# New places for the side stages among 32 scan units, and a last stage that sums four parts behind, in SBUF

## The chip, the cores and the metric

The kernel runs on one core of one Trainium2 chip. The metric is the device time of one execution in microseconds. Its engines are TensorE (PE in the rows; PEld is its weight load), VectorE (DVE), ScalarE (ACT), GpSimd (POOL) and SyncE (SP), which only issues transfers here.

## The reference, cut to what matters

For 32 sequences of 512 tokens with 256 features, in float32:

```
x = x + layernorm(A(layernorm(x)))        # A: a state space block and an attention-like block
x = x + layernorm(F(layernorm(x)))        # F: 8 experts, top 2, capacity 2048 per expert

A:  u, res = split(x @ in_w);  u = silu(conv4(u));  dt, B, C = split(u @ xp_w)
    delta = softplus(dt @ dt_w + dt_b);  dA[t,d,n] = exp(delta * -exp(A_log))
    h[t] = dA[t] * h[t-1] + delta[t] * u[t] * B[t]          # 512 channels x 16 states
    y = sum_n(h * C) + u * D;  m = (y * silu(res)) @ out_w
    h = ln(m + x); q, k; G = sum over tokens of (weights * q); hs = ((G * k) @ proj * ln(h)) @ fl
    h2 = ln(hs + h);  out = ln(gelu(h2 @ d1) @ d2 + h2)
F:  router softmax of the top 2, the first 2048 tokens of each expert kept, relu(x @ w1) @ w2,
    times the router's weight, added back at the token's row
```

The last stage computes `out = x1 + layernorm(F's rows)` for each token, `x1` being the result of the first line.

## The kernel before, in words

It has three phases, one behind the other.

**The attention phase** takes one sequence at a time through a scan. The 512 channels are four chunks of 128 partitions, and the 16 states go in pairs, so a sequence has 4 x 8 = 32 units. In unit k VectorE runs one `tensor_tensor_scan` over two states of 512 steps (L1111) and makes the next unit's input with one multiply, `drive` (L1084; at a chunk's start also `du`, L1079). ScalarE makes the decays of unit k+1 with two exponentials (L745), GpSimd multiplies unit k-1 with C (L529, `times_c`), and TensorE adds unit k-2 into the PSUM tile `y` (L920, preceded at a chunk's start by the skip term, L917). At the end of a chunk VectorE's `gate` (L1090) takes `y` times the gate into `u`. `st` has four buffers, so scan k waits for TensorE's sum of unit k-4; `dA` has two, so the decays of unit k+1 wait for scan k-1. SyncE loads the rows of B and C of unit k+2 (L369), with two buffers for B and four for C.

Beside the scan of sequence b run the side stages of three others: `late` of b-2, `post` of b-1 and `pre` of b+1. `pre` normalises, projects, convolves and makes delta. `post` does all from the output projection to the first half of the feed-forward (d1 and gelu). `late` does its second half (d2), the last normalisations, the first residual, the router, and scatters the tokens to the experts' rows by indirect transfers from GpSimd.

The order on each engine is written out by hand. A sequence has 96 slots, three for a unit. In every slot an engine first does its own piece of the scan and then what the stages have for this slot. VectorE has nothing in slot 3k, scan k in slot 3k+1, `drive` of unit k+1 in slot 3k+2. ScalarE has one decay of unit k+1 in 3k and one in 3k+1, GpSimd `times_c` of unit k-1 in 3k+1, TensorE the sum of unit k-2 in 3k+2, SyncE the row loads of unit k+2 in 3k. What is left of the scan (TensorE's sums 30 and 31, GpSimd's product 31) comes behind slot 95. Each stage is a generator that yields the slot of its next piece from a list `at`:

```python
def run_to(self, slot):
    while self.slot is not None and self.slot <= slot:
        self.slot = next(self.instructions, None)
...
            for slot in range(SLOTS * NU):
                if parts is not None:
                    parts[slot % SLOTS](slot // SLOTS)
                for stage in stages:
                    stage.run_to(slot)
```

The stages of one slot come in the order gates, late, post, pre. Between engines there are only semaphores. Nothing plans these places at build time: the lists `at` are all there is. Two sequences form one turn of a hardware loop (14 turns for sequences 2 to 29), the others stand before and behind it.

Names that the text uses: on VectorE `f_sum0`, `f_sum1` (L1186), `f_g` (L1194, which reads the power `r_late` of GpSimd, L473), the second statistics, `dots` (L1208); "t" (L1165, which reads TensorE's projection `hs` and SyncE's receipt L434); `delta0`, `delta2` (L1066); conv (L1061). On TensorE `m0`, `m1` (output projection), `d2_0` to `d2_3` (all L866), `d1` in four pairs (L992), the turns (L858). On GpSimd `s_g`, `s_b` and the small instructions of a layernorm: a negated mean, variance plus epsilon, a power of -1/2 on 128x4 (L473, L497), a product.

**The expert phase** runs four turns of two experts. It isn't touched.

**The last stage** (`combine_phase`) takes 32 parts of 512 tokens. A part is loaded by SyncE into one of eight tiles `rows` (128x1024), VectorE takes its statistics (L1555, L1560), GpSimd makes scale and shift (L1587 to L1592), ScalarE normalises in four instructions (L1616), the sum with `x1_all`, which lies in SBUF, goes to VectorE for even parts (L1568) and to GpSimd for odd ones (L1601), and ScalarE issues the store (L1623). Even parts are normalised into four PSUM tiles `normed`, odd ones in place. The sum of part n-2 stands ahead of the statistics of part n on VectorE, and ahead of scale and shift of part n on GpSimd; the store of part n-2 behind the normalisation of part n.

Of the kernel before, what the change touches and what calls it, by code (L numbers as in the profile page):

```python
# [12 lines left out]
P = 128  # L13
# [97 lines left out]
def attention_phase(nc, t, env, sem):  # L111
# [14 lines left out]
    with ExitStack() as ctx:  # L126
# [225 lines left out]
        def _(sp):  # L352
# [19 lines left out]
            def pre(b, par):  # L372
                at = iter((2, 16, 52, 64, 95))
# [37 lines left out]
            def post(b, par, more):  # L411
                at = iter((4, 52))
# [13 lines left out]
            def late(b):  # L426
                at = iter((38, 58))
# [13 lines left out]
        def _(pool):  # L441
# [61 lines left out]
            def pre(b, par):  # L503
                at = iter((11, 16, 67, 69, 70, 73))
# [45 lines left out]
            def post(b, par, more):  # L550
                at = iter((13, 19, 22, 34, 37, 41, 53, 53, 61, 70))
# [34 lines left out]
            def late(b):  # L586
                at = iter((0, 1, 18, 20, 22, 27, 29, 43, 43, 45, 45, 45, 45, 48, 51))
# [37 lines left out]
        def _(act):  # L625
# [37 lines left out]
            def pre(b, par):  # L663
                at = iter((10, 14, 17, 17, 19, 19, 25, 36, 43, 43, 48, 55, 59, 59, 59, 60, 61, 62, 65, 66, 69, 92))
# [97 lines left out]
            def post(b, par, more):  # L762
                at = iter((12, 20, 35, 35, 35, 35, 37, 53, 64, 73, 76, 86, 95))
# [57 lines left out]
            def late(b):  # L821
                at = iter((22, 25, 25, 30, 36, 42))
# [26 lines left out]
        def _(pe):  # L849
# [20 lines left out]
            def pre(b, par):  # L870
                at = iter((20, 25, 25, 25, 36, 38, 46, 46, 47, 49, 52, 52, 55, 55))
# [58 lines left out]
            def post(b, par, more):  # L930
                at = iter((1, 2, 24, 26, 26, 44, 48, 54, 61, 67, 76, 78, 83, 84, 88))
# [64 lines left out]
            def late(b):  # L996
                at = iter((0, 10, 10, 13, 38, 38, 45))
# [32 lines left out]
        def _(dve):  # L1030
# [20 lines left out]
            def pre(b, par):  # L1051
                at = iter((20, 28, 33, 39, 82, 88, 95))
# [40 lines left out]
            def gates(b, par):  # L1093
                at = iter((30, 56, 77))
# [28 lines left out]
            def post(b, par, more):  # L1123
                at = iter((2, 11, 11, 27, 31, 44, 49, 58, 68))
# [53 lines left out]
            def late(b):  # L1178
                at = iter((13, 18, 18, 18, 40, 40, 42))
# [300 lines left out]
def combine_phase(nc, t, env, sem):  # L1480
# [3 lines left out]
    with ExitStack() as ctx:  # L1484
# [4 lines left out]
        H = 4  # L1489
# [6 lines left out]
        normed = [ctx.enter_context(nc.psum_tensor(f"normed{i}", [P, TT, D], F32)) for i in range(H)]  # L1496
# [11 lines left out]
        c_out_dve = Steps(sem("c_out_dve"), range(0, G, 2))  # L1508
        c_out_pool = Steps(sem("c_out_pool"), range(1, G, 2))
        c_out = [c_out_dve, c_out_pool]  # L1510
# [35 lines left out]
        def _(dve):  # L1546
# [16 lines left out]
            def add(n, i):  # L1563

                if n % 2:
                    return
                dve.wait_ge(*c_normed.at(n, i))
                dve.tensor_tensor(x1_of(n, i), normed[n // 2 % H][:, :, :].rearrange("p t d -> p (t d)"), x1_of(n, i), ALU.add)\  # L1568
                    .then_inc(c_out_dve.did(n), 1)

            turns(dve, ((2, add), (0, stats)))

        @block.gpsimd
        def _(pool):
# [20 lines left out]
            def add(n, i):  # L1595

                if n % 2 == 0:
                    return
# [5 lines left out]
            turns(pool, ((2, add), (0, scale_and_shift)))  # L1604

        @block.scalar
        def _(act):
            c_normed.credit(act)

            def normalise(n, i):  # L1610
                act.wait_ge(*c_shift.at(f"shift{n}", i))
                if n % 2 == 0:
                    act.wait_ge(*(c_out_dve.at(n - 2 * H, i) if n >= 2 * H else c_out_dve.at((n - 2 * H) % G, i - 1)))
                for tile in range(TT):
                    src = rows[n][:, tile, :]
                    last = act.activation(src if n % 2 else normed[n // 2 % H][:, tile, :], src, ACT.Identity,  # L1616
                                          bias=shift[n][:, tile:tile + 1], scale=r[n][:, tile:tile + 1])
                last.then_inc(c_normed.did(n), 1)

            def store(n, i):  # L1620
                act.wait_ge(*c_out[n % 2].at(n, i))
# [4 lines left out]
            turns(act, ((0, normalise), (2, store)))  # L1626
# [35 lines left out]
```

## Time and profile before

| | us |
|---|---|
| three timed runs | 6304.99, 6323.98, 6331.19 |
| median | 6323.98 |
| the profiled execution, its own time | 6312.81 |
| its span in the trace | 6311.1 |
| VectorE busy, whole span | 5058.4 (80%) |
| TensorE busy | 5337.9 (85%) |
| GpSimd busy | 4465.4 (71%) |
| ScalarE busy | 3688.4 (58%) |
| first and last start of a scan (L1111) | 69.1 and 5468.6 |
| first statistics of the last stage | 6180.3 |

The attention phase is the stretch of the scans and some 100 us behind them. A wait in the rows is the idle time of an engine just before an instruction, with what ended it; "issue" is a wait for nothing that the profile shows, as at the jump of a loop.

### The profile page before, as it was taken

What the parts mean: (1) busy time and instruction counts of PE and PEld (TensorE: products, weight loads), DVE (VectorE), ACT (ScalarE), POOL (GpSimd) and SP (SyncE); (2) the same over time, 40 slices, a digit from 0 to 9 for tenths busy, and PEclk for the clock granted to TensorE, in tenths of its full rate; (3) what the DMA queues carried; (4) which work ended last, traced back from release to release, by engine and by line L of the source; (5) the groups of instructions that cost most, each with busy time, mean ns of one, the idle gap of its engine ahead of it and who ended that gap; (6) DMA issues with size and microseconds to landing.
All of it is one profiled execution on the core that took longest, in us unless ns stands there. A gap on an engine that the chain in (4) does not pass through costs nothing. (4 is left out here: it accounts for less than half of the span.)

```text
span 6311.1 us, 71449 instructions
## 1 busy us (share of the span) xinstructions
PE 5337.9 (85%) x16896; PEld 2976.5 (47%) x16896; DVE 5058.4 (80%) x6651; ACT 3688.4 (58%) x6370; POOL 4465.4 (71%) x3013
## 2 busy tenths in 40 slices
PE   5788888888888888988888888888898888749990
PEld 2344444444444444444444444444444444436660
DVE  5888989998889899898888999988898898612224
ACT  5566666666666666666666666666666665321114
POOL 3677777777777777777777777777777777523446
PEclk8899999999999999999999999999999999869995
DMA  7876666666666666666666666666665666405556
GB/s 223 277 244 228 227 229 228 235 226 219 223 220 226 222 222 223 220 226 222 224 217 227 218 218 216 220 212 218 218 219 201 222 220 213 145 27 119 122 109 220
DMA packets 486058, 1316.23 MB, mean 209 GB/s; under 512 B 54687, under 2 KB 194976, under 8 KB 485552
## 3 DMA queue, kind: packets, MB, share of 16 engines
q1 hardware_dynamic: 441424, 1242.65, 58.4%
q0 software_dynamic: 30720, 34.17, 3.0%
q10 hardware_dynamic: 13408, 34.08, 1.4%
q14 instruction: 361, 2.96, 0.2%
q8 instruction: 145, 2.38, 0.2%
HBM read 1189.94 MB, written 138.02 MB: 210 GB/s over the span
## 5 line engine op out<-in xcount | busy, mean ns | idle before, releaser
L529 POOL TENSOR_TENSOR st<-st,C_rows 128x1024 f32<-128x1024 f32 x1024 | 2478.7, 2427 | 520.1 <-DVE st L1111 509.9
L1111 DVE TENSOR_TENSOR_SCAN st<-dA,drive 128x1024 f32<-128x1024 f32 x1024 | 2338.9, 2284 | 242.4 <-PE y L920 117.1
L920 PE MATMUL y<-st,ident 128*128 128x512 f32 x4096 | 1974.4, 620 | 171.6 <-POOL st L529 168.4
L745 ACT ACTIVATE dA<-delta,a_neg 128x511 f32<-128x511 f32 x2048 | 1367.8, 712 | 706.8 <-DVE st L1111 698.1
L920 PEld LDWEIGHTS y<-st,ident 128*128 128x128 f32 x4096 | 793.3, 199 | 1193.7 <-issue 865.4
L1084 DVE TENSOR_TENSOR drive<-du,B_rows 128x1024 f32<-128x1024 f32 x1024 | 1260.2, 1231 | 107.5 <-DVE du L1079 20.7
L889 PE MATMUL pre_bank<-e_abs,in_w 128*128 128x512 f32 x1024 | 587.9, 715 | 86.2 <-DVE u L1061 78.1
L866 PE MATMUL post_bank<-d_w,gT 128*128 128x256 f32 x2048 | 464.2, 383 | 30.3 <-issue 29.6
L617 POOL DMA_INDIRECT expert_in<-tb,idx x256 | 271.8, 1062 | 264.0 <-DVE idx L1266 190.7
L866 PEld LDWEIGHTS post_bank<-d_w,gT 128*128 128x128 f32 x2048 | 391.9, 192 | 129.0 <-issue 77.1
L1427 POOL DMA_INDIRECT token_rows<-O,dest_i x128 | 198.1, 1547 | 307.2 <-DVE O L1474 219.9
L889 PEld LDWEIGHTS pre_bank<-e_abs,in_w 128*128 128x128 f32 x1024 | 214.5, 223 | 351.2 <-issue 206.3
L1061 DVE SCALAR_TENSOR_TENSOR u<-pre_bank,conv_w,u 128x511 f32<-128x511 f32 (+2 forms) x384 | 285.8, 744 | 23.7 <-ACT u L690 14.7
L992 PE MATMUL post_bank<-F,d_w 128*128 128x512 f32 x512 | 245.9, 625 | 2.5 <-ACT F L811 1.5
L858 PE MATMUL post_bank<-ident,tb 128*128 128x128 f32 x768 | 116.7, 301 | 142.3 <-ACT tb L646 109.0
L866 PE MATMUL post_bank<-F,gT 128*128 128x256 f32 x512 | 153.1, 466 | 98.2 <-ACT F L799 98.2
L1377 PE MATMUL bank<-XT,w 128*128 128x512 f32 x512 | 227.8, 598 | 5.3 <-ACT XT L1402 5.3
L1387 PE MATMUL bank<-w,I 128*128 128x256 f32 x1024 | 228.6, 381 | 3.3 <-issue 3.3
L992 PE MATMUL pre_bank<-F,d_w 128*128 128x512 f32 x512 | 230.2, 592 | 0.0
L866 PE MATMUL pre_bank<-out_w,u 128*128 128x256 f32 x1024 | 226.4, 379 | 2.5 <-issue 2.5
L1474 DVE TENSOR_SCALAR O<-bank,w_slot 128x256 f32<-128x256 f32 x128 | 53.1, 477 | 213.9 <-PE bank L1387 213.9
L1410 ACT ACTIVATE I<-bank 128x512 f32<-128x512 f32 x64 | 38.2, 597 | 316.6 <-PE bank L1377 316.6
(210 smaller groups left out, 8048.9 us busy)
## 6 DMA issues: line engine op xcount, KB each, us to landing
B_rows<-bc_rows SPq DMA_DIRECT2D x1024, 512.0 KB
C_rows<-bc_rows SPq DMA_DIRECT2D x1024, 512.0 KB, 5.1
expert_in<-zeros ACTq DMA_DIRECT2D x22, 768.0 KB, 5.5
X<-expert_in SPq DMA_DIRECT2D x32, 528.0 KB, 4.8
xin<-in_x SPq DMA_DIRECT2D x32, 512.0 KB, 6.9
xn_rows<-xin SPq DMA_DIRECT2D x32, 512.0 KB, 3.3
token_rows<-zeros SPq DMA_DIRECT2D x32, 512.0 KB, 7.4
h<-xn_rows SPq DMA_DIRECT2D x32, 512.0 KB, 7.8
```

The lines of the kernel that those rows point to most:

```text
L529: pool.tensor_tensor(tile[:, :, :], tile[:, :, :], bc[1][k % ROWS[1]][:, :, :], ALU.mult)\
L617: pool.indirect_dma_start(out=xe_dram, out_offset=bass.IndirectOffsetOnAxis(ap=idx[:, tile, choice:choice + 1], axis=0), in_=tb_wide[:, ti ...
L745: return act.activation(dA[k % 2][:, j, 1:L], delta[par][:, c, 1:L], ACT.Exp, scale=a_neg[:, c, n:n + 1])
L866: last = pe.matmul(banks[tile // 2][:, (tile % 2) * D:(tile % 2 + 1) * D], srcT[:, c, tile * P:(tile + 1) * P], w[:, c, :], start=c == 0, ...
L889: last = pe.matmul(RB[m % 2][:, :], in_w[:, c, m * P:(m + 1) * P], xT[:, c, :], start=c == 0, stop=c == KD - 1)
L920: last = pe.matmul(Y[:, :], ident[:, :], st[k % RING][:, j, :], start=False, stop=pair == CU - 1 and j == 1)
L992: last = pe.matmul(FB[j % 4][:, :], d1_w[:, c, j * P:(j + 1) * P], F[:, c, :], start=c == 0, stop=c == KD - 1)
L1061: dve.scalar_tensor_tensor(late, RB[c % 2][:, 0:L - 1 - j], conv_w[:, c, 2 - j:3 - j], late, ALU.mult, ALU.add).then_inc(pre_dve.did(f"con ...
L1084: dve.tensor_tensor(DR[:, :, :], DU[:, :].unsqueeze(1).to_broadcast([P, 2, L]), bc[0][k % ROWS[0]][:, :, :], ALU.mult).then_inc(scan_in.di ...
L1111: dve.tensor_tensor_scan(st[k % RING][:, :, :].rearrange("p a l -> p (a l)"), dA[k % 2][:, :, :].rearrange("p a l -> p (a l)"), DR[:, :, : ...
L1377: last = pe.matmul(MB[m][:, 0:BLK], w1[e][:, c, m * P:(m + 1) * P], XT[n % 2][:, c, :], start=c == 0, stop=c == KD - 1)
L1387: last = pe.matmul(OB[tile // 2][:, (tile % 2) * D:(tile % 2 + 1) * D], I[n % 2][:, c, tile * P:(tile + 1) * P], w2[e][:, c, :], start=c = ...
```

## The change

Every list `at` of the attention phase gets other numbers; the pieces and their order within a stage stay. In the last stage `normed` goes, ScalarE normalises every part in place, the sum follows four parts behind, and GpSimd has one sum of four, VectorE three.

```diff
 sync     pre   (2, 16, 52, 64, 95)                     -> (4, 39, 86, 95, 95)
          post  (4, 52)                                 -> (1, 35)
          late  (38, 58)                                -> (25, 51)
 gpsimd   pre   (11, 16, 67, 69, 70, 73)                -> (12, 14, 78, 80, 86, 88)
          post  (13, 19, 22, 34, 37, 41, 53, 53, 61, 70)
             -> (18, 27, 32, 36, 47, 48, 50, 65, 67, 78)
          late  (0, 1, 18, 20, 22, 27, 29, 43, 43, 45, 45, 45, 45, 48, 51)
             -> (10, 11, 21, 24, 27, 28, 32, 41, 41, 41, 45, 45, 45, 47, 48)
 scalar   pre   (10, 14, 17, 17, 19, 19, 25, 36, 43, 43, 48, 55, 59, 59, 59, 60, 61, 62, 65, 66, 69, 92)
             -> (9, 11, 14, 14, 18, 31, 32, 47, 50, 53, 60, 65, 65, 65, 66, 66, 71, 73, 74, 74, 83, 95)
          post  (12, 20, 35, 35, 35, 35, 37, 53, 64, 73, 76, 86, 95)
             -> (16, 22, 28, 32, 38, 40, 40, 56, 69, 76, 78, 88, 94)
          late  (22, 25, 25, 30, 36, 42)                -> (26, 28, 29, 34, 34, 40)
 tensor   pre   (20, 25, 25, 25, 36, 38, 46, 46, 47, 49, 52, 52, 55, 55)
             -> (11, 17, 29, 31, 39, 44, 47, 51, 52, 55, 61, 61, 61, 63)
          post  (1, 2, 24, 26, 26, 44, 48, 54, 61, 67, 76, 78, 83, 84, 88)
             -> (5, 5, 20, 25, 29, 36, 50, 59, 65, 68, 80, 83, 86, 89, 95)
          late  (0, 10, 10, 13, 38, 38, 45)             -> (0, 11, 11, 11, 36, 36, 39)
 vector   pre   (20, 28, 33, 39, 82, 88, 95)            -> (31, 37, 43, 44, 95, 95, 95)
          gates (30, 56, 77)                            -> (32, 55, 75)
          post  (2, 11, 11, 27, 31, 44, 49, 58, 68)     -> (0, 9, 10, 26, 34, 48, 49, 65, 73)
          late  (13, 18, 18, 18, 40, 40, 42)            -> (12, 18, 19, 20, 38, 39, 40)
```

```diff
-        H = 4
+        LAG = 4
-        normed = [ctx.enter_context(nc.psum_tensor(f"normed{i}", [P, TT, D], F32)) for i in range(H)]
+        c_out_dve = Steps(sem("c_out_dve"), [n for n in range(G) if n % 4 != 1])
+        c_out_pool = Steps(sem("c_out_pool"), [n for n in range(G) if n % 4 == 1])
             def load(n, i):
-                if n % 2:
-                    sp.wait_ge(*c_out_pool.at(n, i - 1))
-                else:
-                    sp.wait_ge(*c_normed.at(n, i - 1))
+                sp.wait_ge(*c_out(n).at(n, i - 1))
             def add(n, i):                                  # VectorE
-                if n % 2:
+                if n % 4 == 1:
                     return
-                dve.tensor_tensor(x1_of(n, i), normed[n // 2 % H]..., x1_of(n, i), ALU.add)
+                dve.tensor_tensor(x1_of(n, i), rows[n]..., x1_of(n, i), ALU.add)
-            turns(dve, ((2, add), (0, stats)))
+            turns(dve, ((LAG, add), (0, stats)))
             def add(n, i):                                  # GpSimd
-                if n % 2 == 0:
+                if n % 4 != 1:
                     return
-            turns(pool, ((2, add), (0, scale_and_shift)))
+            turns(pool, ((LAG, add), (0, scale_and_shift)))
             def normalise(n, i):
-                if n % 2 == 0:
-                    act.wait_ge(*(c_out_dve.at(n - 2 * H, i) if ... else ...))
-                    last = act.activation(src if n % 2 else normed[n // 2 % H][:, tile, :], src, ...)
+                    last = act.activation(src, src, ...)
-            turns(act, ((0, normalise), (2, store)))
+            turns(act, ((0, normalise), (LAG, store)))
```

## Rows read from the trace of the kernel before

**Rows 1.** Windows: us, then busy us (x instructions) per engine, PEclk, DMA share, GB/s

```profile
2000.00:3000.00 1000.00, 881.87 (x2760) 481.38 (x2759) 894.78 (x1087) 654.58 (x1133) 772.52 (x504) 0.95 0.66 224
```

**Rows 2.** Groups by line, 1000 to 3000 us: busy us, mean ns, idle before

```profile
L1111 DVE TENSOR_TENSOR_SCAN st<-dA,drive 128x1024 f32<-128x1024 f32 x379 | 865.8, 2284 | 87.9 <-PE y L920 45.8 <-issue 13.3 <-ACT dA L745 13.0
...
L694 ACT ACT_TABLE_LOAD x11 | 14.1, 1283 | 0.2
```

**Rows 3.** Timeline of VectorE, one unit with nothing beside it: start, us, what

```profile
3060.30 1.23 DVE L1084 TENSOR_TENSOR drive<-du,B_rows 128x1024 f32<-128x1024 f32 x1
...
3064.02 1.23 DVE L1084 TENSOR_TENSOR drive<-du,B_rows 128x1024 f32<-128x1024 f32 x1
```

**Rows 4.** Waits of VectorE, 1000 to 5000 us: total us, times, longest

```profile
DVE st L1111 <- PE y L920: 86.2, 64, 2.9
DVE post_bank L1194 <- POOL r_late L473: 38.0, 24, 1.6
DVE st L1111 <- ACT dA L745: 33.5, 50, 3.3
DVE tb L1165 <- PE post_bank L866: 32.9, 15, 3.3
DVE st L1111 <- issue: 27.7, 11, 3.9
...
DVE tb L1165 <- SPq L434: 17.0, 9, 2.0
...
DVE drive L1084 <- issue: 1.0, 5, 0.2
```

**Rows 5.** Timeline of VectorE around the late stage

```profile
3118.01 2.29 DVE L1111 TENSOR_TENSOR_SCAN st<-dA,drive 128x1024 f32<-128x1024 f32 x1 [0.84 <-ACT dA L745]
...
3125.81 1.67 DVE L1194 SCALAR_TENSOR_TENSOR post_bank<-post_bank,mv_late,row_ln_g 128x256 f32<-128x256 f32 x4 [1.58 <-POOL r_late L473]
```

**Rows 6.** Timeline of VectorE around "t"

```profile
3034.78 1.66 DVE L1165 SCALAR_TENSOR_TENSOR tb<-post_bank,rk,row_pr_b 128x256 f32<-128x256 f32 x4 [2.12 <-PE post_bank L866]
...
3039.39 2.29 DVE L1111 TENSOR_TENSOR_SCAN st<-dA,drive 128x1024 f32<-128x1024 f32 x1 [1.82 <-PE y L920]
```

**Rows 7.** Timeline of the last stage: GpSimd at its start, VectorE's sums later

```profile
6182.65 0.25 POOL L1587 TENSOR_SCALAR c_shift<-c_mv 128x4 f32<-128x4 f32 x1 [6.08 <-DVE c_mv L1560]
...
6184.70 0.23 POOL L1587 TENSOR_SCALAR c_shift<-c_mv 128x4 f32<-128x4 f32 x1
...
6270.42 1.23 DVE L1568 TENSOR_TENSOR x_all<-normed,x_all 128x1024 f32 x1 [2.73 <-ACT normed L1616]
...
6278.14 1.22 DVE L1568 TENSOR_TENSOR x_all<-normed,x_all 128x1024 f32 x1 [2.84 <-ACT normed L1616]
```

**Rows 8.** Groups by line, 6170 to 6311 us

```profile
L1555 DVE BATCH_NORM_STATS2 c_stat<-rows 128x6 f32<-128x256 f32 x128 | 44.3, 409 | 15.8 <-DMA rows<-token_rows 15.8
...
L1560 DVE BATCH_NORM_AGGREGATE c_mv<-c_stat 128x2 f32<-128x6 f32 x128 | 12.2, 157 | 4.7
```

**Rows 9.** Timeline of TensorE

```profile
3061.39 3.56 PE L920 MATMUL y<-st,ident 128*128 128x512 f32 x4 [1.10 <-POOL st L529]
...
3069.07 3.60 PE L920 MATMUL y<-st,ident 128*128 128x512 f32 x8
...
3108.62 7.07 PE L866 MATMUL post_bank<-d_w,gT 128*128 128x256 f32 x32
```

**Rows 10.** Timeline of VectorE, scan 0 behind the jump of the loop

```profile
3093.12 2.29 DVE L1111 TENSOR_TENSOR_SCAN st<-dA,drive 128x1024 f32<-128x1024 f32 x1 [2.27 <-issue]
```

**Rows 11.** Timeline of VectorE and GpSimd: a delta beside a C multiply, then one alone

```profile
3071.66 1.20 DVE L1066 SCALAR_TENSOR_TENSOR delta<-delta,e_abs 128x1024 f32<-128x1024 f32 x1
...
3071.83 3.25 POOL L529 TENSOR_TENSOR st<-st,C_rows 128x1024 f32<-128x1024 f32 x1 [1.24 <-DVE st L1111]
...
3076.46 2.36 POOL L529 TENSOR_TENSOR st<-st,C_rows 128x1024 f32<-128x1024 f32 x1 [1.38 <-DVE st L1111]
```

**Rows 12.** Window in the last stage, columns as in rows 1

```profile
6240.00:6260.00 20.00, 0.00 (x0) 0.00 (x0) 13.48 (x51) 10.30 (x20) 14.47 (x25) 0.50 0.76 269
```

More of the change, by code:

```diff
@@ L372, in pre @@
             def pre(b, par):
-                at = iter((2, 16, 52, 64, 95))
+                at = iter((4, 39, 86, 95, 95))
                 yield next(at)
@@ L411, in post @@
             def post(b, par, more):
-                at = iter((4, 52))
+                at = iter((1, 35))
                 yield next(at)
@@ L426, in late @@
             def late(b):
-                at = iter((38, 58))
+                at = iter((25, 51))
                 yield next(at)
@@ L503, in pre @@
             def pre(b, par):
-                at = iter((11, 16, 67, 69, 70, 73))
+                at = iter((12, 14, 78, 80, 86, 88))
                 yield next(at)
@@ L550, in post @@
             def post(b, par, more):
-                at = iter((13, 19, 22, 34, 37, 41, 53, 53, 61, 70))
+                at = iter((18, 27, 32, 36, 47, 48, 50, 65, 67, 78))
                 yield next(at)
@@ L586, in late @@
             def late(b):
[L587 removed]
+                at = iter((10, 11, 21, 24, 27, 28, 32, 41, 41, 41, 45, 45, 45, 47, 48))
                 yield next(at)
@@ L762, in post @@
             def post(b, par, more):
-                at = iter((12, 20, 35, 35, 35, 35, 37, 53, 64, 73, 76, 86, 95))
+                at = iter((16, 22, 28, 32, 38, 40, 40, 56, 69, 76, 78, 88, 94))
                 yield next(at)
@@ L821, in late @@
             def late(b):
-                at = iter((22, 25, 25, 30, 36, 42))
+                at = iter((26, 28, 29, 34, 34, 40))
                 yield next(at)
@@ L870, in pre @@
             def pre(b, par):
-                at = iter((20, 25, 25, 25, 36, 38, 46, 46, 47, 49, 52, 52, 55, 55))
+                at = iter((11, 17, 29, 31, 39, 44, 47, 51, 52, 55, 61, 61, 61, 63))
                 yield next(at)
@@ L996, in late @@
             def late(b):
-                at = iter((0, 10, 10, 13, 38, 38, 45))
+                at = iter((0, 11, 11, 11, 36, 36, 39))
                 for tile in range(TT):
@@ L1051, in pre @@
             def pre(b, par):
-                at = iter((20, 28, 33, 39, 82, 88, 95))
+                at = iter((31, 37, 43, 44, 95, 95, 95))
                 for c in range(KI):
@@ L1093, in gates @@
             def gates(b, par):
-                at = iter((30, 56, 77))
+                at = iter((32, 55, 75))
                 for c in range(KI - 1):
@@ L1123, in post @@
             def post(b, par, more):
-                at = iter((2, 11, 11, 27, 31, 44, 49, 58, 68))
+                at = iter((0, 9, 10, 26, 34, 48, 49, 65, 73))
                 yield next(at)
@@ L1178, in late @@
             def late(b):
-                at = iter((13, 18, 18, 18, 40, 40, 42))
+                at = iter((12, 18, 19, 20, 38, 39, 40))
                 for i in range(2):
@@ L1507, in combine_phase, with c_out @@
         c_normed = Steps(sem("c_normed"), range(G))
-        c_out_dve = Steps(sem("c_out_dve"), range(0, G, 2))
-        c_out_pool = Steps(sem("c_out_pool"), range(1, G, 2))
-        c_out = [c_out_dve, c_out_pool]
+        c_out_dve = Steps(sem("c_out_dve"), [n for n in range(G) if n % 4 != 1])
+        c_out_pool = Steps(sem("c_out_pool"), [n for n in range(G) if n % 4 == 1])
+        def c_out(n):
+            return c_out_pool if n % 4 == 1 else c_out_dve
         def turns(engine, parts):
@@ L1563, in add @@
             def add(n, i):
-                if n % 2:
+                if n % 4 == 1:
                     return
                 dve.wait_ge(*c_normed.at(n, i))
-                dve.tensor_tensor(x1_of(n, i), normed[n // 2 % H][:, :, :].rearrange("p t d -> p (t d)"), x1_of(n, i), ALU.add)\
+                dve.tensor_tensor(x1_of(n, i), rows[n][:, :, :].rearrange("p t d -> p (t d)"), x1_of(n, i), ALU.add)\
                     .then_inc(c_out_dve.did(n), 1)
-            turns(dve, ((2, add), (0, stats)))
+            turns(dve, ((LAG, add), (0, stats)))
         @block.gpsimd
@@ L1611, in normalise @@
                 act.wait_ge(*c_shift.at(f"shift{n}", i))
-                if n % 2 == 0:
-                    act.wait_ge(*(c_out_dve.at(n - 2 * H, i) if n >= 2 * H else c_out_dve.at((n - 2 * H) % G, i - 1)))
                 for tile in range(TT):
                     src = rows[n][:, tile, :]
-                    last = act.activation(src if n % 2 else normed[n // 2 % H][:, tile, :], src, ACT.Identity,
-                                          bias=shift[n][:, tile:tile + 1], scale=r[n][:, tile:tile + 1])
+                    last = act.activation(src, src, ACT.Identity, bias=shift[n][:, tile:tile + 1],
+                                          scale=r[n][:, tile:tile + 1])
                 last.then_inc(c_normed.did(n), 1)
             def store(n, i):
-                act.wait_ge(*c_out[n % 2].at(n, i))
+                act.wait_ge(*c_out(n).at(n, i))
                 act.sem_inc(carried_act_c, 1)
```

4 lines of the change are left out of this document (2 added, 2 removed).

## The prediction, on record before the change was run

> **What bounds the kernel now.** I read four views in this order: the busy time of each engine in one steady stretch, the groups by line for the length of a sequence, the waits of VectorE over the steady part, and the timeline around each wait. In the steady stretch VectorE is busy for 895 of 1000 us and TensorE for 882, ScalarE for 655, GpSimd for 773 [rows 1]. Two engines are close to full, and what an order of the work can win is the time in which VectorE stands. 379 scans in 2000 us [rows 2] are 11.84 sequences, 168.9 us each. A unit with nothing beside it takes 3.72 us from one drive multiply to the next [rows 3], 119 us for 32 units; the rest is side stages and waits.
>
> VectorE's waits from 1000 to 5000 us (23.7 sequences) come in 20 rows that add up to 327 us, 13.8 us a sequence ([rows 4] has the largest and the last). About 2.2 us of that lies between two dependent instructions of one stage and stays. 1.2 us (27.7/23.7) is the loop's jump. That leaves 10.4 us a sequence, the most that a better order could win. Much of it sits in two places. In units 5 and 6 the late stage does its sum, statistics, normalisation and second statistics in one slot and stands 1.58 us for GpSimd's power; a scan before it is late too [rows 5]. In units 18 and 19 the "t" multiply stands for TensorE's projection, and the scan after it for TensorE's sum [rows 6].
>
> The last stage is a ring of latencies. Two VectorE sums are 7.72 us apart [rows 7], so a part takes 3.86 us, though VectorE works only 1.84 us of statistics per part (44.3 and 12.2 us for 32 parts, and the gaps) [rows 8] and 1.23 us of sum every second part: sum(n) stands behind normalise(n), and statistics(n+2) stand behind sum(n).
>
> **The slots, part by part.** The attention stage gets and loses no instruction but some table loads; places in each engine's order change. So each item is worth what it does to a wait.
>
> *Late stage on VectorE* (18, 18, 18 to 18, 19, 20). A scan of 2.29 us now lies between the statistics and the first use of the power, whose wait was 1.58: gone in every sequence (38.0/23.7 = 1.6 us). Scans wait 86.2+33.5 us for TensorE and ScalarE [rows 4], 5.1 a sequence; the places shown have 0.84 and 1.82 of it, and I give 1.8 to the lump, 1.9 to "t" and the rest to the end of a sequence. With the lump cut by a scan and a drive I take 1.3 of the 1.8 as gone. *"t"* goes from slot 58 to 65 while the projection goes from 54 to 59: the distance grows from 4 slots to 6, and SP's receipt moves from 58 to 51, so 32.9+17.0 us (2.1 a sequence) go, and the scan behind it mostly too. *Router pieces* 40, 40, 42 to 38, 39, 40: a scan now covers TensorE's count, 0.2 us.
>
> *What comes back.* TensorE's d2 tiles cost 3.5 us each (7.07 for two) and a unit's sum about 1.75 (two in 3.6) [rows 9]. m0 and m1 now stand at slot 5, so TensorE does d2_0, m0, m1 (10.6 us), sum 0 (2.6 with the skip term), sum 1 and d2_1 in a row: d2_1 is done 17.9 us after scan 0 starts, VectorE wants it at 17.4. I count 0.6. ScalarE's slot 14 stands for the turn that TensorE does behind d2_3, at about 26 us; copies and two decays follow: scan 6 is about 0.5 us late. GpSimd's s_g and s_b (two of 2.36) now stand before x_m, for which ScalarE's squares wait: decay 5 is ready at 21, wanted at 22, so this costs nothing while TensorE is on time. conv 2 and 3 share unit 14; tap3 comes 2.2 us after scan 14's end, wanted at 3.5. Silu is split over slots 50 and 53: two more table loads of 1.28 us [rows 2]; ScalarE's 345 us of idle in 1000 cover them, and if the cover is gone they are 2.6 us. Gate 2 (slot 75) comes two slots before TensorE's sum 23 (77): 0.5 us. SP's zero rows, a 512 KB write, go from 52 to 86, into units of 3.72 us, and the copy of xd to DRAM from 64 to 95, ahead of the first row loads; these rows are wanted some 10 us later. I add 0.3 us for rows that land late.
>
> *The boundary.* delta0, delta2 (were 82, 88) and the next drive all stand at 95, and gate 3, before in slot 2, now stands ahead of scan 0. VectorE's own work from the end E of scan 31 to scan 0 is 2.3 + 2.1 + 0.6 = 5.0 us. Gate 3 needs TensorE's sum 31. From unit 25 on TensorE has seven sums (12.2) and four pairs of d1 (3.5 each), 26.2 us, from 2.5 us behind scan 25's end, and VectorE reaches E in 6 x 3.72 = 22.3. So sum 31 ends at E+6.4, scan 0 starts at E+7.1: 2.1 us of standing. In return the loop's jump, 2.27 us in every second sequence [rows 10], lies under this wait.
>
> One more thing sits there. Where delta runs beside GpSimd's C multiply, that multiply takes 3.25 us, and 2.36 elsewhere [rows 11]: it stood until delta, which reads two SBUF operands, was through. Two deltas and du in a row hold the multiply of unit 31 back by 1 to 3 us, so sum 31 ends between E+5.3 and E+7.2. I take 0.4 us more.
>
> Sum: waits of 10.4 and the jump's 1.2 become 0.6 + 0.5 + 0.5 + 0.3 + 2.5 = 4.4, plus 0.4 for which I find no cause to strike them: 6.8 us a sequence. But this reckoning takes TensorE at its faster level. A sum takes 3.56 us instead of 1.75 where the clock is at half (1.2 GHz) [rows 9], and a mean granted clock of 0.95 [rows 1] is a tenth of the time at half, 17 us a sequence, up to 8 us of TensorE's work. The old waits contain that, mine don't. I take 2.8 us for it, between 0 and 7, nearer the low end since only part of it falls where VectorE is waiting. Gain 4.0 us a sequence, bounds 0 to 7, in 29 sequences that have all stages: **116 us, bounds 0 to 200**. The first and last sequences, where a chain runs alone, I leave at nothing, 10 us either way.
>
> **The last stage.** Ahead of statistics(n) now stands sum(n-4), so the latency chain of 7.7 us spans four parts and no longer binds. What does, per four parts: VectorE 4 x 1.84 + 3 x 1.2 = 11.0; GpSimd 4 x 2.05 (four small instructions with their gaps, one part to the next at the stage's start [rows 7]) + 2.36 = 10.6; ScalarE less than either; transfers: 1 MB in 3.86 us keeps the DMA engines busy for 0.76 [rows 12], so 2.9 us a part if full, 11.7 for four. The lower bound is 2.9 us a part: 32 x 0.95 = 30 us gained. But VectorE's sum no longer reads PSUM: both operands are in SBUF, the pair of [rows 11]. If each of three sums stops GpSimd for its whole 1.2, four parts take 10.6 + 3.6 = 14.2 us, 3.5 a part, 11 us gained. A power (1.04 of the small ones) may run on beside a sum, so I take 3.15 us a part: **22 us gained, bounds 11 and 30**. A load now waits for the sum, not the normalisation; the ring of eight leaves about four parts, 12 us, for it, so nothing.
>
> The Trainium skill ("SBUF — State Buffer", section "SBUF: two separate sides") states that a VectorE instruction with two SBUF inputs and a GpSimd instruction that reads SBUF exclude each other for the whole instruction, whichever came first. By that rule the last stage would gain the 11 us, not 22, and a sum of VectorE would also stand behind GpSimd's.
>
> **Sum.** The profiled execution took 6312.8 us, 6311.1 of them span. 6312.8 - 116 - 22 = 6175. The three timed runs lie at 6305 to 6331, median 6324, 0.2% above the profiled one; I forecast 6180.
>
> **The rivals.**
> *A, slower: the boundary.* All engines meet behind scan 31, and gate 3 makes scan 0 wait for TensorE's last sum, with d1_6 and d1_7 ahead of the sums of units 30 and 31. Whatever TensorE is late in units 25 to 31 goes straight into the sequence; before, four st buffers hid it. If a quarter of its 26.2 us runs at half clock, 6.6 us come on top: 29 x (6.6 - 4.0) = +75, less 22: 6366, 6370 as a median. It decides from 4.8 us a sequence. For it: TensorE's 882 of 1000. Against: a clock of 0.95.
> *B, the waits move.* TensorE's 150 us of work stay, and VectorE waits for them elsewhere; or most places had slack and moving them does nothing. Attention is unchanged, the last stage gives 22: 6302. For it: the wait for PE y is the largest. Against: the 1.58 us gets its cover by construction.
> *C, slots as forecast, last stage held by the shared port* at 3.5 us or more a part, 0 to 11 us gained: 6197. For it: the stretched multiply [rows 11].
>
> **Chances.** Forecast 0.50, C 0.18, B 0.20, A 0.12. A measurement tells about 0.5% here, 32 us. Faster takes the forecast, C and 0.07 of B: 0.75. Same 0.12, slower 0.13. Range: down to 6090 (7 us a sequence and all of the last stage), up to 6305 (B's middle).
>
> **What would show it.** Right: a sequence of 163 to 167 us; no wait of L1194 for r_late; those of "t" gone; a new wait of the gate (u<-y) for PE y once a sequence, 2 to 3 us, the jump inside it; a C multiply of over 4 us beside two deltas; a last stage of 98 to 115 us from first statistics to the end, with GpSimd's small instructions stretched beside sums. Wrong: 168 us or more; a gate wait of over 7 us; 3.8 us a part in the last stage; table or row loads ahead of scans.

## The result, and the profile after

The changed kernel takes **6479.2 us** (median of 6, 6463.1 to 6484.4) where the kernel before takes 6320.7 (median of 6): ratio 1.0249, 95% interval 1.0231 to 1.0267. It is slower by 2.5%, where 6180 (6090 to 6305) was forecast. The profiled execution has a span of 6479.3 us, before 6311.1.

I split both spans at the scans. "Sequence" is the mean distance of sequences 2 to 29, "last stage" the time from its first statistics to the end:

| us | before | after | forecast |
|---|---|---|---|
| sequence | 169.7 | 176.9 | 165.7 |
| last stage | 130.8 | 115.6 | 109 |
| span | 6311.1 | 6479.3 | 6173 |

So the last stage gave 15 us, and each sequence takes 7.3 us more. Everything that needs explaining lies in the sequence.

TensorE's granted clock fell as well, from a mean of 0.926 of full speed to 0.907. That isn't what costs the time: experiment 2 below runs at 0.912 and is some 205 us faster than the changed kernel.

Names in what follows: q·w_g are four products of q with a row of weights, made on VectorE with a `tensor_tensor_reduce` (L1150); G is TensorE's sum with these weights (L966), and `ssg` (L1159) VectorE's reduction of what TensorE adds up behind G. ssk is TensorE's sum of k squared (L958), the count its running count of tokens for each expert, `cum` (L1246) VectorE's read of it. li_g and li are GpSimd's scale and shift of a normalised tile (L543, L547), `dv` (L1220) a subtraction on 128x4 in the router.

First the waits of VectorE after the change, 1000 to 5000 us (22.6 sequences; total us, times, longest), as in [rows 4]:

```profile
DVE st L1111 <- PE y L920: 73.9, 50, 3.5
DVE ssg L1159 <- PE post_bank L968: 45.2, 23, 4.7
DVE cum L1246 <- PE post_bank L1023: 39.5, 22, 2.0
DVE u L1090 <- issue: 29.4, 12, 3.8
...
DVE st L1111 <- ACT dA L745: 16.3, 43, 0.8
...
DVE u L1090 <- PE y L920: 1.5, 4, 0.9
```

The waits for `r_late` (38.0) and for the "t" projection and its receipt (32.9 and 17.0) are gone, as forecast. All rows of this view add up to 268 us, 11.9 a sequence, against 13.8 before. VectorE stands *less* than before, and yet a sequence is longer. The time must be in its busy part, which the windows show too (columns as in [rows 1]; kernel after):

```profile
2000.00:3000.00 1000.00, 855.37 (x2645) 466.60 (x2646) 904.50 (x1081) 642.82 (x1091) 731.54 (x483) 0.92 0.63 213
```

VectorE ran 1081 instructions where it ran 1087 before [rows 1], and was busy for 905 us where it was for 895. The change gives VectorE no new instruction in this phase, so some must have become longer. The groups by line of VectorE, 1000 to 5000 us (total busy us, mean ns, idle before), of the kernel before:

```profile
L1079 DVE TENSOR_TENSOR du<-delta,u 128x512 f32<-128x512 f32 x94 | 63.4, 675 | 0.0
L1066 DVE SCALAR_TENSOR_TENSOR delta<-delta,e_abs 128x1024 f32<-128x1024 f32 x48 | 57.6, 1199 | 0.0
...
L1150 DVE CUSTOM_DVE_ANT_0 gT<-gT,row_w_g 128x256 f32<-128x256 f32 x92 | 33.4, 419 | 0.0
L1220 DVE TENSOR_TENSOR dv<-top 128x4 f32<-128x4 f32 x23 | 24.8, 1078 | 0.0
```

and of the kernel after:

```profile
L1150 DVE CUSTOM_DVE_ANT_0 gT<-gT,row_w_g 128x256 f32<-128x256 f32 x90 | 184.1, 2096 | 0.0
L1066 DVE SCALAR_TENSOR_TENSOR delta<-delta,e_abs 128x1024 f32<-128x1024 f32 x46 | 103.2, 2285 | 0.0
L1079 DVE TENSOR_TENSOR du<-delta,u 128x512 f32<-128x512 f32 x90 | 97.9, 1087 | 0.8
...
L1220 DVE TENSOR_TENSOR dv<-top 128x4 f32<-128x4 f32 x22 | 3.2, 146 | 0.0
```

Same instructions, same shapes, other durations. By the means, a sequence pays on L1150 (the four products q·w_g) 4 x (2.096 - 0.419) = 6.7 us, on the two deltas 2.2, on the four halves of du 1.6, and gets 0.9 back on dv: **9.6 us more**. Less the 1.9 us of waits that is 7.7, where 7.3 were measured. All three that grew read both operands from SBUF. `drive` and the scan, which read one operand from PSUM (the tiles du and `drive`), kept their 1.23 and 2.28 us in both kernels, though GpSimd's C multiplies run beside them all the time. The idle column beside them says 0.0: whoever reads only the waits doesn't see this at all.

What stretches them is seen in the timeline of all engines (start, us, what), kernel after, behind scan 15:

```profile
3116.00 2.36 POOL L543 TENSOR_TENSOR gT<-gT,row_lni_g 128x1024 f32<-128x1024 f32 x1
3116.43 2.23 DVE L1150 CUSTOM_DVE_ANT_0 gT<-gT,row_w_g 128x256 f32<-128x256 f32 x1
...
3118.59 0.42 DVE L1150 CUSTOM_DVE_ANT_0 gT<-gT,row_w_g 128x256 f32<-128x256 f32 x1
...
3118.93 5.57 DVE L1150 CUSTOM_DVE_ANT_0 gT<-gT,row_w_g 128x256 f32<-128x256 f32 x1
3119.57 2.36 POOL L547 TENSOR_TENSOR gT<-gT,row_lni_b 128x1024 f32<-128x1024 f32 x1
3121.86 2.35 POOL L529 TENSOR_TENSOR st<-st,C_rows 128x1024 f32<-128x1024 f32 x1
...
3124.43 0.41 DVE L1150 CUSTOM_DVE_ANT_0 gT<-gT,row_w_g 128x256 f32<-128x256 f32 x1
...
3125.18 3.14 PE L966 MATMUL post_bank<-qw,gT 128*128 128x1 f32 x14 [8.62 <-DVE ssk L1156]
...
3129.22 0.16 DVE L1159 TENSOR_REDUCE ssg<-post_bank 128x1 f32<-128x4 f32 x1 [1.84 <-PE post_bank L968]
```

The first product, 0.42 us long by itself, ends at 3118.66, 0.3 us after GpSimd's li_g, which had begun 0.4 us before it. The second, while GpSimd issues an indirect DMA, takes its 0.42. The third is recorded as 5.57 us: it ends at 3124.50, 0.3 us after the second of two GpSimd instructions (li and the C multiply of unit 15, which followed at once) that run on unhindered at 2.36 us each. This pattern stands in 27 of the 32 sequences. In two of the other five (products from 2943.87 and from 5417.96 us) GpSimd has only indirect DMAs at that moment, and all four products take 0.41 to 0.47 us: the same slots, without the stretch. The reason is in the lists `at`: VectorE's q·w_g went from slot 44 to 48 and GpSimd's li_g and li from 37 and 41 to 47 and 48. Before, only indirect DMAs of GpSimd's ran beside q·w_g.

One thing in these rows stays unexplained. The third product's record begins 0.63 us before that of li, and 0.42 us would have been enough for it. So the records don't show that li came first here; GpSimd's spans are rough, and what held the product between 3119.0 and 3119.57 isn't known.

TensorE, too, stood 8.6 us for the products. Its granted clock was 1.00 from 3105 to 3116.5, and 0.50 (1.2 GHz) from 3125.18 to 3128.32, when it did G: 348 ns a matmul on average, before 247. The slow G is most of the new wait of `ssg`, 45.2/22.6 = 2.0 us a sequence.

The same at the end of a sequence, where two deltas stand in a row (after, same view):

```profile
3195.79 4.49 DVE L1066 SCALAR_TENSOR_TENSOR delta<-delta,e_abs 128x1024 f32<-128x1024 f32 x2
...
3195.95 3.24 POOL L529 TENSOR_TENSOR st<-st,C_rows 128x1024 f32<-128x1024 f32 x1 [0.92 <-DVE st L1111]
...
3198.82 3.60 PE L920 MATMUL y<-st,ident 128*128 128x512 f32 x8
...
3200.31 0.70 DVE L1079 TENSOR_TENSOR du<-delta,u 128x512 f32<-128x512 f32 x1
...
3201.21 1.23 DVE L1084 TENSOR_TENSOR drive<-du,B_rows 128x1024 f32<-128x1024 f32 x1 [0.20 <-DVE du L1079]
...
3204.38 0.69 DVE L1090 TENSOR_TENSOR u<-y,g 128x512 f32<-128x512 f32 x1 [1.94 <-issue]
```

The first delta held the multiply for 0.9 us, as it does in [rows 11]; when it ended the multiply ran, and the second delta took the other 3.3 of the 4.49 us. Scan 31 ended at 3195.87. VectorE was ready for gate 3 at 3202.44 and TensorE had sum 31 at 3202.42: in this kernel the two come out level, and here the jump of the loop follows on top.

### The profile page after: what moved, and what is told of

It is laid out like the page before. It is cut to its first block and busy times, and to the rows that moved or that the text cites. A ratio compares the mean times of both kernels' runs of the same rounds, so it can differ in the third digit from the quotient of the medians.

```text
span 6479.3 us, 71499 instructions
## 1 busy us (share of the span) xinstructions
PE 5397.7 (83%) x16896; PEld 3017.9 (47%) x16896; DVE 5334.9 (82%) x6659; ACT 3783.3 (58%) x6432; POOL 4441.3 (69%) x3005
## 5 line engine op out<-in xcount | busy, mean ns | idle before, releaser
L920 PE MATMUL y<-st,ident 128*128 128x512 f32 x4096 | 2013.4, 628 | 150.9 <-POOL st L529 150.9
L889 PE MATMUL pre_bank<-e_abs,in_w 128*128 128x512 f32 x1024 | 572.0, 693 | 132.0 <-DVE u L1061 128.6
L966 PE MATMUL post_bank<-qw,gT 128*128 128x1 f32 x512 | 107.4, 340 | 236.2 <-DVE ssk L1156 230.6
L1150 DVE CUSTOM_DVE_ANT_0 gT<-gT,row_w_g 128x256 f32<-128x256 f32 x128 | 238.3, 1913 | 1.3 <-ACT gT L792 1.3
L992 PE MATMUL post_bank<-F,d_w 128*128 128x512 f32 x512 | 232.9, 598 | 1.5 <-ACT F L811 1.5
```

The costliest lines, as they stand in the source:

```text
L889: last = pe.matmul(RB[m % 2][:, :], in_w[:, c, m * P:(m + 1) * P], xT[:, c, :], start=c == 0, stop=c == KD - 1)
L920: last = pe.matmul(Y[:, :], ident[:, :], st[k % RING][:, j, :], start=False, stop=pair == CU - 1 and j == 1)
L992: last = pe.matmul(FB[j % 4][:, :], d1_w[:, c, j * P:(j + 1) * P], F[:, c, :], start=c == 0, stop=c == KD - 1)
L1150: last = dve.tensor_tensor_reduce(out=junk_dve[:, tile, :], in0=q[:, tile, :], in1=rows["w_g"][:, :], scale=D ** -0.5, scalar=0.0, op0=ALU ...
```

## The experiments

**1. The last stage alone.** The new last stage with all old slots; the edit is the other way round, every list `at` as before:

```diff
-                at = iter((4, 39, 86, 95, 95))
+                at = iter((2, 16, 52, 64, 95))
...
-                at = iter((0, 9, 10, 26, 34, 48, 49, 65, 73))
+                at = iter((2, 11, 11, 27, 31, 44, 49, 58, 68))
```

> The old lists of slots with the new last stage. Theory (the slots are what made it slower): the scans take 5402 us from first to last as before, the last stage 115.6 us from its first statistics to the end as in the changed kernel against 130.8 before, total 6321 - 15 = 6306, ratio 0.9976. Rival (the change of the last stage reaches back, through code or memory placement): the scans get longer too, total above 6330.

Measured: 6301.5 us, ratio 0.9985 (0.9971 to 1.0000), sequence 170.1, last stage 116.0. The two halves of the change are independent: the stage gives its 15 us here as well (the whole kernel is 0.15% faster by the ratio), and the slots cost the rest.

**2. q·w_g five slots earlier** in the changed kernel:

```diff
-                at = iter((0, 9, 10, 26, 34, 48, 49, 65, 73))
+                at = iter((0, 9, 10, 26, 34, 43, 49, 65, 73))
```

> The changed kernel with one piece moved: the weighted sums of q (L1150) on VectorE in slot 43, right behind scan 14, instead of 48. Theory (shared port: these four instructions read two SBUF operands and stand behind GpSimd's li_g, li and C products): L1150 falls from 8.1 to 1.7 us a sequence, the wait of ssg for TensorE (2.0) goes, total 6479 - 29 x 8.4 = 6235, at most 6310 if other waits take a part. Rival 1 (the lists are too tight for TensorE): L1150 is short but VectorE waits instead, total within 1% of 6479. Rival 2 (the instruction is slow by itself while other engines use the gT tile): L1150 stays above 4 us a sequence.

Measured: 6270.7 us, ratio 0.9924 (0.9905 to 0.9942), sequence 169.3. One integer is worth 3.25% by the two ratios, some 205 us. But slot 43 isn't free either; the groups by line of VectorE for this kernel, 1000 to 5000 us:

```profile
L1150 DVE CUSTOM_DVE_ANT_0 gT<-gT,row_w_g 128x256 f32<-128x256 f32 x92 | 95.0, 1086 | 0.0
L1079 DVE TENSOR_TENSOR du<-delta,u 128x512 f32<-128x512 f32 x95 | 86.1, 906 | 0.8
```

One product a sequence still takes 3.2 us, beside a C multiply only; 1.7 us a sequence for all four had been expected, and it is 4.3.

**3. The deltas spread** over slots 91 and 94 in the changed kernel:

```diff
-                at = iter((31, 37, 43, 44, 95, 95, 95))
+                at = iter((31, 37, 43, 44, 91, 94, 95))
```

> The changed kernel with delta0 and delta2 right behind scans 30 and 31 (slots 91 and 94) instead of both in 95. Theory (shared port: the second delta stands behind GpSimd's C product of unit 31, which got in between): both deltas take 1.2 us, 2.2 us a sequence less, total 6479 - 31 x 2.2 = 6411. Rival (gate 3 waits for TensorE's sum 31 anyway): the deltas are short, the gate waits 2 us longer, total within 15 us of 6479.

Measured: 6483.8 us, ratio 1.0267 (1.0242 to 1.0291), sequence 177.0: no gain. The recorded rival had this total, but not the way to it: the gate's wait for TensorE is 0.2 us a sequence. The timeline of this kernel says why:

```profile
3185.97 5.64 POOL L529 TENSOR_TENSOR st<-st,C_rows 128x1024 f32<-128x1024 f32 x2
...
3187.70 1.71 DVE L1066 SCALAR_TENSOR_TENSOR delta<-delta,e_abs 128x1024 f32<-128x1024 f32 x1
...
3192.84 1.20 DVE L1066 SCALAR_TENSOR_TENSOR delta<-delta,e_abs 128x1024 f32<-128x1024 f32 x1
3194.07 2.73 DVE L1079 TENSOR_TENSOR du<-delta,u 128x512 f32<-128x512 f32 x1
```

Delta2 is back at 1.20 us, and the wait passed to the next instruction with two SBUF operands, du: 2.73 us where it takes 0.67. Over the sequence du went from a mean of 1087 to 1602 ns (4 x 0.515 = 2.1 us) while the deltas fell from 2285 to 1457 (1.7 us). Of two such instructions back to back beside GpSimd's multiply, the second pays; which one it is doesn't matter. The first rows show something else: the delta of 3187.70 ran between two C multiplies that GpSimd had in a row (together 5.64 us, 0.9 more than twice 2.36), so it waited for the first of them only. That is so in 31 sequences.

**4. li_g and li cut short.** GpSimd's multiply li_g and its addition li work on one column of 256 in the changed kernel (the rest of li's scale and shift is left out; the edit of li is alike):

```diff
-                times("li_g", li, rows["lni_g"])
+                pool.tensor_tensor(li[:, :, 0:1], li[:, :, 0:1], rows["lni_g"][:, 0:1]...
```

> The changed kernel with GpSimd's li_g and li cut to one column of 256: the rest of the scale and shift of li is left out. Theory (shared port): the first of the four L1150 falls from 2.2 to 0.4 us since li_g is gone, and the third from 5.6 to 0.4 to 3 us, what is left being the C product alone; a sequence 4 to 6 us shorter. Rival (L1150 is slow for another reason): it keeps 8 us a sequence.

Measured in a single run: 6380.7 us, sequence 173.5, 3.4 us less where 4 to 6 were expected. Groups by line of VectorE, 1000 to 5000 us (its lines are shifted by 2, so L1152 is L1150):

```profile
L1068 DVE SCALAR_TENSOR_TENSOR delta<-delta,e_abs 128x1024 f32<-128x1024 f32 x46 | 103.3, 2286 | 0.0
L1081 DVE TENSOR_TENSOR du<-delta,u 128x512 f32<-128x512 f32 x92 | 100.3, 1091 | 0.8
L1152 DVE CUSTOM_DVE_ANT_0 gT<-gT,row_w_g 128x256 f32<-128x256 f32 x92 | 91.5, 1048 | 0.0
```

Of the 6.7 us of stretch 4.2 went with VectorE's own order untouched (4 x (2.096 - 1.048), of which 3.4 arrived); what stays, 2.5 us, is the C multiply of unit 15. So it is GpSimd's work beside the products, not their slot as such.

**5. q·w_g eight slots earlier**, at 40 instead of 48; **6. the same with the deltas at 88 and 91**:

```diff
-                at = iter((31, 37, 43, 44, 95, 95, 95))
+                at = iter((31, 37, 43, 44, 88, 91, 95))
...
-                at = iter((0, 9, 10, 26, 34, 48, 49, 65, 73))
+                at = iter((0, 9, 10, 26, 34, 40, 49, 65, 73))
```

> The changed kernel with the weighted sums of q in slot 40, behind scan 13, where GpSimd is about to issue three scatters and reads no large SBUF tile. Theory (shared port): L1150 at 1.7 us a sequence (8.1 in the changed kernel, 4.2 in slot 43), du of unit 15 falls by 0 to 1 us, total 6271 - 31 x 2.6 = 6190, 6160 to 6200. Rival (TensorE and GpSimd are what bounds, VectorE's stretches only hide it): total stays at 6260 or more.

> The same with delta0 and delta2 in slots 88 and 91, right behind scans 29 and 30, so that no two instructions with two SBUF inputs follow each other behind scan 31. Theory (shared port; in the run with 91 and 94 the wait only passed from the second delta to du): deltas 2.4 and du 2.7 to 3.6 us a sequence, 2.2 us a sequence gained, 6190 - 68 = 6122. Rival (gate 3 waits for GpSimd's product 31 and TensorE's sum 31): the gate's wait grows by what the deltas lose, total within 15 us of the run without it.

Measured: number 5 takes 6204.3 us, ratio 0.9834 (0.9813 to 0.9856), sequence 166.5; number 6 takes 6274.7, 0.9946 (0.9930 to 0.9963), 169.4. Number 5 is a little above the 6160 to 6200 that were expected. Number 6 should have gained 68 us on it, or by its rival come out level; it lost 70, which neither had. In number 5 the products are whole again (groups by line, as above):

```profile
L1079 DVE TENSOR_TENSOR du<-delta,u 128x512 f32<-128x512 f32 x97 | 67.9, 700 | 0.8
...
L1150 DVE CUSTOM_DVE_ANT_0 gT<-gT,row_w_g 128x256 f32<-128x256 f32 x96 | 35.1, 421 | 1.5
```

Against the changed kernel that is 6.7 + 1.5 us of busy time; `ssg` waits 0.9 us less and scans 1.6 less for TensorE: 10.7, and 10.5 were measured. With this one list entry the new slots are 3.2 us a sequence better than the old ones, where 4.0 were forecast for them.

Number 6 answers what the boundary costs. The waits of VectorE in it, 1000 to 5000 us (23.6 sequences):

```profile
DVE u L1090 <- PE y L920: 68.7, 25, 3.0
...
DVE h L1131 <- PE pre_bank L866: 22.4, 12, 3.3
DVE post_bank L1186 <- PE post_bank L866: 18.4, 24, 1.3
```

With the deltas ahead of scans 30 and 31 gate 3 stands 2.9 us a sequence for TensorE's sum 31 (the loop's jump, 1.2 a sequence, now lies under that), and the work behind it another 1.7 for TensorE's m1 and d2, where it was 0.3. In all, 3 us a sequence are lost. This experiment moves the deltas but doesn't take their stretch away: the mean is still 2155 ns, the first standing behind GpSimd's last piece of softplus, L521. So what the stretch costs at slot 95 was not measured. In number 5, VectorE is ready for gate 3 on average 6.6 us after the end of scan 31, and sum 31 is there after 6.5: without the 2.2 us of stretch VectorE would only stand. But in every second sequence the jump follows, gate 3 comes after 8.9 us, and the stretch isn't covered. By these figures it costs some 1.1 us a sequence on average, an estimate that no run tests.

**7. Four edits together, and 8. the last stage with PSUM operands.** Number 7 is number 6 plus TensorE's ssk at 39 instead of 36, plus the edit of number 8, which is made on the old slots: ScalarE writes the normalised part for VectorE's sums into one of three PSUM tiles, so that these sums read one operand from SBUF and one from PSUM. GpSimd's quarter stays in SBUF; the lag of four parts and the one sum in four on GpSimd stay as in the changed kernel. A load into `rows` waits for the normalisation again, not for the sum. The core of the edit, against the changed last stage:

```diff
+        normed = [ctx.enter_context(nc.psum_tensor(f"normed{i}", [P, TT, D], F32)) for i in range(3)]
...
-                sp.wait_ge(*c_out(n).at(n, i - 1))
+                if n % 4 == 1:
+                    sp.wait_ge(*c_out_pool.at(n, i - 1))
+                else:
+                    sp.wait_ge(*c_normed.at(n, i - 1))
...
-                dve.tensor_tensor(x1_of(n, i), rows[n][:, :, :].rearrange("p t d -> p (t d)"), x1_of(n, i), ALU.add)\
+                dve.tensor_tensor(x1_of(n, i), in_psum(n)[:, :, :].rearrange("p t d -> p (t d)"), x1_of(n, i), ALU.add)\
...
+                if n % 4 != 1:
+                    act.wait_ge(*(c_out_dve.at(n - 4, i) if n >= 4 else c_out_dve.at(n + 4, i - 1)))
```

> The run before with two more edits: TensorE's sums of k squared (ssk) in slot 39 behind the count instead of 36, so that VectorE's wait for the count (1.7 us a sequence) goes, and the last stage with VectorE's operand back in PSUM (three tiles). Theory: 29 x 1.7 = 50 us and 8 to 13 us of the last stage less than the run before, 6060 if that is at 6122. Rival (TensorE is the bound by now): less than 15 us from the slots.

> The old slots with a last stage that sums four parts behind with one of four on GpSimd, like the changed kernel, but with VectorE's operand in three PSUM tiles. Theory (shared port stretches GpSimd in the last stage: 613 ns for 235, 3188 for 2343): these return to 0.24 and 2.35 us, the last stage takes 98 to 108 us instead of 115.6. Rival (transfers bound it): 113 to 116 us.

Number 8, a single run: 6290.8 us, and a last stage of 96.4 us instead of 116.0. The groups by line of the last stage, kernel after (6345 to 6480 us):

```profile
L1566 DVE TENSOR_TENSOR x_all<-rows,x_all 128x1024 f32 (+1 forms) x24 | 31.6, 1316 | 16.7 <-ACT rows L1612 15.7 <-issue 0.7
L1599 POOL TENSOR_TENSOR x_all<-rows,x_all 128x1024 f32 (+1 forms) x8 | 25.5, 3188 | 0.7
L1585 POOL TENSOR_SCALAR c_shift<-c_mv 128x4 f32<-128x4 f32 x32 | 19.6, 613 | 11.3 <-DVE c_mv L1558 7.5 <-ACT rows L1612 2.4 <-issue 0.4
```

and of number 8 (6171 to 6300 us):

```profile
L1573 DVE TENSOR_TENSOR x_all<-normed,x_all 128x1024 f32 (+1 forms) x24 | 29.3, 1219 | 4.0 <-ACT normed L1621 3.1 <-issue 0.7
L1606 POOL TENSOR_TENSOR x_all<-rows,x_all 128x1024 f32 (+1 forms) x8 | 18.8, 2346 | 0.7
L1592 POOL TENSOR_SCALAR c_shift<-c_mv 128x4 f32<-128x4 f32 x32 | 7.5, 233 | 12.7 <-DVE c_mv L1565 8.0 <-ACT normed L1621 1.3 <-issue 1.1
```

A GpSimd sum of 2.34 us took 3.19 beside VectorE's, and an instruction on 4 columns 0.61 on average instead of 0.23 (0.9 to 1.3 where it met a sum). With one operand in PSUM both are gone. GpSimd saves 4 x 0.38 + 0.84 = 2.4 us per four parts, which is what four parts gain: the stage divided by its 32 parts is 3.0 us instead of 3.6. The earlier loads are not the reason: VectorE's statistics stand 19.5 us for a load in the whole stage of the changed kernel, and 16.1 in number 8.

Number 7: 6201.3 us, ratio 0.9828 (0.9807 to 0.9848), last stage 96.6, sequence 167.3. It was expected at 6060. Against number 6 it is 73 us better, 19 of them in the last stage; but it is no better than number 5, which has neither the ring nor the moved ssk: spreading the deltas gave back what these won.

**9. The best version**: the changed kernel with q·w_g at 40, ssk at 39, the deltas left at 95, and the PSUM tiles:

```diff
-                at = iter((5, 5, 20, 25, 29, 36, 50, 59, 65, 68, 80, 83, 86, 89, 95))
+                at = iter((5, 5, 20, 25, 29, 39, 50, 59, 65, 68, 80, 83, 86, 89, 95))
...
-                at = iter((0, 9, 10, 26, 34, 48, 49, 65, 73))
+                at = iter((0, 9, 10, 26, 34, 40, 49, 65, 73))
```

> The changed kernel with q's weighted sums in slot 40, TensorE's ssk in slot 39, VectorE's operand of the last stage in PSUM, and the deltas left in slot 95. Theory: the deltas in 95 cost nothing that TensorE's last sum wouldn't cost anyway, so the sequence falls from 166.5 us (q's sums alone) by up to the 1.7 us of the count's wait, and the last stage takes 96.5 us: 6204 - 19 - 30 x (0.5 to 1.7) = 6134 to 6170. Rival (TensorE bounds the sequence, so nothing comes of slot 39): 6185.

Measured: **6131.7 us**, ratio 0.9693 (0.9655 to 0.9730), sequence 165.3, last stage 96.8. It beats the kernel before by 3.1% and the changed one by some 5%. Its largest waits of VectorE, 1000 to 5000 us (24.2 sequences):

```profile
DVE st L1111 <- PE y L920: 69.3, 51, 3.4
DVE u L1090 <- issue: 28.9, 12, 3.3
DVE drive L1084 <- DVE du L1079: 18.8, 97, 0.2
DVE st L1111 <- ACT dA L745: 16.1, 43, 0.6
```

The wait of `cum` for the count, 1.75 us a sequence in the changed kernel, is gone. It stood there because TensorE had ssk in slot 36, whose bank VectorE frees in slot 38 (the read of the dots): 3.57 us of ssk and a sum of 3.76 then lay ahead of the count that VectorE wants in slot 40. With ssk behind the count that order is undone. Part of it came back as more waiting for TensorE's sums (1.7 to 2.9 us a sequence).

## Why the prediction was wrong

**The step that failed** stands at the head of its slots part: since the stage gets and loses no instruction but table loads, "each item is worth what it does to a wait". An instruction's own duration was taken as fixed wherever it was put. For q·w_g, li_g and li the prediction has no term at all; they were costed at nothing, and they cost 6.7 us of products, and most of 2.0 us of `ssg` behind them, each sequence. 29 x (6.7 + 2.0) = 252 us. The single entry of experiment 5 gave back 4.15% by the two ratios, 262 us (with 1.5 us of du a sequence in it, and 1.1 of `ssg` still there).

The evidence was at hand. [Rows 11] show the pair, delta and a C multiply, and I read it in one direction only: GpSimd stood, VectorE didn't. That VectorE's came first there was chance. And the dv of the kernel before, a subtraction of 4 columns with a mean of 1078 ns, showed the other direction 23 times; I never looked for an instruction that takes longer than its size. The Trainium skill ("SBUF — State Buffer", section "SBUF: two separate sides") states that the two exclude each other whichever came first. The trace agrees in both directions: the multiply takes 3.24 instead of 2.36 behind a delta that began 0.16 us before it, the first product 2.23 instead of 0.42 behind li_g, which began 0.42 us before it. The third product, 5.57 us, doesn't settle the order, since its record begins before li's. I quoted that rule and let it count in the last stage and, with 0.4 us, at the boundary, instead of going with it through all 96 slots.

**Point by point.**
- *Late stage and "t"*: right. The waits for `r_late`, the projection and the receipt are gone.
- *Router pieces*, "a scan now covers TensorE's count, 0.2 us": wrong. The wait of `cum` went from 0.2 to 1.75 us a sequence, since ssk was moved ahead of the count and waits for the dots; I followed VectorE's places there and not what TensorE had queued.
- *The boundary*: TensorE's side was right, sum 31 ends 6.4 us after scan 31, as forecast. VectorE's side wasn't: its work up to gate 3 takes 6.6 us and not 4.4 (the forecast's 5.0 less the gate's own 0.6), because the second delta is stretched by 2.2. So the forecast wait of 2.1 to 2.8 us, the sign that was to show it, is 1.5 us in 4000. That experiment 6 has a wait of 2.9 there doesn't confirm the sum: its deltas are elsewhere, and sum 31 ends 4.8 us after scan 31. The loop's jump, struck from the sum at 1.2 us a sequence since it was to lie under this wait, stayed (29.4/22.6 = 1.3 us). The forecast "C multiply of over 4 us beside two deltas" was wrong as well, 3.24: GpSimd gets in between the two, and the second delta pays.
- *Sequence 163 to 167 us*: 176.9, and 166.5 with the one entry moved. That this is 3.2 us a sequence where 4.0 were forecast is partly luck: the boundary's wait did not come, while the jump, the wait of `cum` and that of `ssg` did, and the sum had none of these three.
- *Last stage*, 22 us gained within 11 to 30: 15. The term was mis-sized: from the statistics of part 8 to those of part 28 a part takes 3.34 us, where 3.15 were forecast and 3.84 stood before, and the stage's end, from the last part's statistics on, grew from 14.6 to 18.7 us. I let a power run on beside a sum (it did, 1.04 us), but the small instruction ahead of it often took 0.7 to 1.1 us more, and GpSimd's own sum 0.9. By the rule of the Trainium skill the prediction had 11 us, which was nearer than my 22, on the other side. Without the clash the stage gives 34 us, over my upper bound.
- *Rivals*: A named slower and 6370, by TensorE at the boundary. The sign came true and the mechanism did not. C named the shared port in the last stage, which was right, but with 0 to 11 us gained, and it was 15. None of them had VectorE stretched within the sequence.

**Left open.** In the best version scans wait 2.9 us a sequence for TensorE's sums against 1.7 in experiment 5, and I didn't try which piece should move for it. Why the third product is held over two of GpSimd's instructions while the delta of experiment 3 gets in between two wasn't found, nor was a kernel run in which the deltas at slot 95 are whole.

## What to carry to other kernels

When stages are moved against each other, go slot by slot through what VectorE and GpSimd do at the same time, and price every VectorE instruction with two SBUF operands as its own time plus what is left of GpSimd's instruction there, and at worst plus all that GpSimd has in a row. Compare the mean duration of each line between two traces before the waits: this loss stands as busy time, with 0.0 in the idle column. Where the pair can't be parted in time, put one operand in PSUM.

## What the runs showed of the hardware

- The stretch is recorded as work, not as a wait: a VectorE product of 0.42 us stands as 2.23 us behind li_g, and as 5.57 us when GpSimd has li and a C multiply in a row (the second started 0.07 us before the end of the first).
- In that place VectorE wasn't let in between GpSimd's two, in 27 sequences of the changed kernel. That is no rule: in experiment 3 a delta ran between two C multiplies in a row in 31 sequences (1.71 us, the second multiply 3.34), and in experiment 6 one between L521 and a C multiply. Two deltas in a row let GpSimd in between in every run with both at slot 95 (3.24 us for the multiply, 1.20 and 3.3 for the deltas).
- It isn't size that counts: GpSimd's instruction on 4 columns went from 0.23 to between 0.9 and 1.3 us beside a sum, and VectorE's dv on 4 columns from 0.15 to a mean of 1.08 in its old place.
- Products ran whole while GpSimd issued an indirect DMA: the second one here (0.42 us at 3118.59, the DMA from 3118.53 to 3119.54), and in the kernel before, where such DMAs are all that runs beside the products, the 92 of them from 1000 to 5000 us have a mean of 419 ns. Whether the last part of such a DMA held the third product, which should have been done by 3119.4, is open.
- TensorE's G, behind 8.6 us in which it stood, took 348 ns a matmul instead of 247, at a granted clock of 0.50, where it had been 1.00 before it stood. Here a stall of VectorE was followed by slower work of the engine that waited for it.
